# A vision tower's embedding and attention loop: pixel copies image by image, in eight pieces on ScalarE and VectorE instead of three on ScalarE and GpSimd

## The reference

```python
def _L0_tok_ref(img, w, b, patch_size):          # img: (64, 3, 224, 224)
    patches = img.reshape(B, C, Hp, p, Wp, p)    # p = 16, Hp = Wp = 14: 196 tokens an image
    patches = patches.transpose(0, 2, 4, 1, 3, 5).reshape(B, S, C * p * p)
    out = jnp.einsum('bsk,ek->bse', patches, w) + b
    return out
...
h = _L0_tok_ref(x, L0_tok_w, L0_tok_b, 16)
h = h + _L0_attn_ref(_layernorm(h, axis=-1), L0_attn_Wq, L0_attn_Wk, L0_attn_Wv)
h = h + _L0_ffn_ref(_layernorm(h, axis=-1), ...)     # top-k experts
h = h + _L1_attn_ref(_layernorm(h, axis=-1), ...)
h = h + _L1_ffn_ref(_layernorm(h, axis=-1), ...)     # routed experts
```

## Time and profile before

| | |
|---|---|
| median of 3 runs | 2328.66 us (2323.18 to 2329.88) |
| the profiled execution | 2333.29 us, span 2331.6 us |
| busy over the span | PE 79%, PEld 57%, DVE 57%, ACT 52%, POOL 50% |
| mean granted TensorE clock | 0.904 |

### The profile page before, as it was taken

One profiled execution on the slowest core, in us unless ns is written; L12 is line 12 of the kernel. 1 busy time (PEld: TensorE's weight loads), 2 busy tenths in 40 slices (PEclk: granted clock), 3 DMA queues, 4 the chain that ended last, 5 costly groups with the idle time before them and its releaser, 6 DMA issues. The chain is left out here.

```text
span 2331.6 us, 48836 instructions
## 1 busy us (share of the span) xinstructions
PE 1835.8 (79%) x12709; PEld 1328.7 (57%) x12710; DVE 1339.7 (57%) x5135; ACT 1211.4 (52%) x2915; POOL 1161.9 (50%) x1035
## 2 busy tenths in 40 slices
PE   5888888872158874998797979797988459998996
PEld 3555555551136552665565656565655359998985
DVE  3788888855541104888777777777776422222222
ACT  2555555530025432876666666666665135555553
POOL 2344444413038872245545454545454448777776
PEclk8999999985569886999999999999999679999998
DMA  9777777610014332011111111111111057776775
GB/s 205 176 191 188 189 189 189 181 29 15 19 45 71 62 46 64 23 40 41 39 34 39 35 38 35 38 35 38 34 34 29 25 118 137 134 136 122 134 134 84
DMA packets 271687, 198.98 MB, mean 85 GB/s; under 512 B 26121, under 2 KB 251947, under 8 KB 271531
## 3 DMA queue, kind: packets, MB, share of 16 engines
q1 hardware_dynamic: 221547, 161.65, 26.8%
q0 software_dynamic: 49984, 35.38, 11.0%
HBM read 144.12 MB, written 52.80 MB: 84 GB/s over the span
## 5 line engine op out<-in xcount | busy, mean ns | idle before, releaser
L2123 POOL DMA_INDIRECT out_dram<-r_yw,r_idx x212 | 328.4, 1549 | 114.9 <-issue 50.4
L2015 POOL DMA_INDIRECT rows_scratch<-routed_row,slot_u x256 | 268.8, 1050 | 124.7 <-issue 72.8
L1691 ACT ACTIVATE a_probsT<-a_p_sc 98x392 f32<-98x392 f32 x384 | 191.9, 500 | 128.0 <-PE a_p_sc L1520 108.0
L2191 ACT ACTIVATE r_hT<-r_p_up,r_b1T 128x256 f32<-128x256 f32 x424 | 190.0, 474 | 115.0 <-PE r_p_up L2165 111.6
L2152 PEld LDWEIGHTS r_p_y<-w_all,r_hT 128*128 128x128 f32 x1696 | 223.3, 192 | 11.1
L2152 PE MATMUL r_p_y<-w_all,r_hT 128*128 x1696 | 224.2, 275 | 0.0
L2165 PE MATMUL r_p_up<-r_xgT,r_w1e 128*128 128x256 f32 x848 | 220.5, 383 | 0.7 <-ACT r_xgT L2196 0.6
L1517 PE MATMUL a_p_sc<-q_head,kT 128*98 128x392 f32 x512 | 218.9, 509 | 0.5 <-ACT q_head L1718 0.5
L407 PE MATMUL p_embed<-pix,w_pix 96*128 96x392 f32 x512 | 211.1, 520 | 4.8 <-ACT pix L533 4.8
L1718 ACT ACTIVATE q_head<-qT,head_of 128x196 f32<-128x196 f32 x512 | 197.1, 467 | 0.0
L650 POOL TENSOR_SCALAR vare<-mv 98x4 f32<-98x4 f32 x64 | 27.9, 436 | 296.9 <-DVE mv L628 215.7
(11 more groups left out here) (361 smaller groups left out, 4535.0 us busy)
## 6 DMA issues: line engine op xcount, KB each, us to landing
img<-in_x_dram SPq DMA_DIRECT2D x192, 196.0 KB, 3.6
img<-in_x_dram SPq DMA_DIRECT2D x192, 189.0 KB, 3.7
r_w1e<-in_L_ffn_W_dram SPq DMA_DIRECT2D x106, 256.0 KB, 3.0
r_xg<-rows_scratch SPq DMA_DIRECT2D x106, 130.0 KB
xn_scratch<-xn SPq DMA_DIRECT2D x32, 196.0 KB
h_scratch<-h SPq DMA_DIRECT2D x32, 196.0 KB
h<-h_scratch SPq DMA_DIRECT2D x32, 196.0 KB
h3b<-h_scratch SPq DMA_DIRECT2D x32, 196.0 KB
```

Source lines behind the costliest of these rows:

```text
L1691: act.activation(probsT[:, r3, m, b * 2 * PAIR:(b + 1) * 2 * PAIR], p_sc[i % 2][:, 0:2 * PAIR], ACT.Exp).then_inc(exped, 1)
L2015: pool.indirect_dma_start(rows_dram, bass.IndirectOffsetOnAxis(ap=slot_u[:, k % 2, c, t:t + 1], axis=0), row[:, k % 2, c, t, :], None).the ...
L2123: pool.indirect_dma_start(acc_dram, bass.IndirectOffsetOnAxis(ap=idx[:, (k - 3) % 4, t:t + 1], axis=0), yw[:, (k - 3) % 4, t, :], None, co ...
L2191: act.activation(hT[:, (k - 1) % 2, f, :], p_up[f][:, 0:G], ACT.Silu, bias=b1T[:, bass.ds(e * FC + f, 1)]).then_inc(act_h, 1)
```

## The change

Each image's half of the buffer is loaded by itself, with a semaphore of its own. The pixel copies are done image by image, in pairs of columns: eight pieces of 2 x 196 elements a unit. ScalarE does pairs 0 and 1 of each image, VectorE pairs 2 and 3; GpSimd does none. The pieces stand between the other work of these engines. TensorE's `patch` waits for all eight pieces of the unit each time that it is called. On ScalarE `hT` moves ahead of the exponentials. VectorE's `emit` now runs one iteration longer, since its pieces are of the unit ahead, and GpSimd's one shorter.

```diff
-        def load_images(sp, u, k):
-            for m in range(2):
-                dst = img[:, k % 2, m, :].rearrange("r (g w) -> r g w", g=GRID)
...
+        img_loaded = [[sem(f"img_loaded{k}_{m}") for m in range(2)] for k in range(2)]
+        def load_image(sp, u, k, m):
...
@@ emit_sp
-                    wait(sp, pix_ready, n - 1, apart=True)
-                    wait(sp, pix_ready_pool, 2 * (n - 1))
-                    load_images(sp, n, k)
+                    for m in range(2):
+                        copied = PAIRS * (n - 2) + 2 * (m + 1)
+                        wait(sp, pix_act, copied, apart=True)
+                        wait(sp, pix_dve, copied)
+                        load_image(sp, n, k, m)
@@ patch
                 if 0 in js:
-                    wait(pe, pix_ready, n + 1)
                     wait(pe, hT_ready, n)
-                if half // 2 in js:
-                    wait(pe, pix_ready_pool, 2 * n + 2)
+                wait(pe, pix_act, PAIRS * (n + 1))
+                wait(pe, pix_dve, PAIRS * (n + 1))
@@ new, called by emit_act and emit_dve
+        def copied_pixels(copy, eng, done_sem, n, k, m, pair):
+            if not live(n, 0, UNITS):
+                return
+            if pair % 2 == 0:
+                wait(eng, img_loaded[k % 2][m], (n // 2 + 1) * 16 * 6 if isinstance(n, int) else
+                     (n - (k % 2)) * (16 * 3) + 16 * 6, apart=True)
+                wait(eng, embedded, n - 1, apart=True)
+            js, q = slice(2 * pair, 2 * pair + 2), slice(m * TOKENS, (m + 1) * TOKENS)
+            in_columns = img[:, k % 2, m].rearrange("r (q j) -> r j q", j=PATCH)
+            copy(pix[:, k % 2, js, q], in_columns[:, js, :]).then_inc(done_sem, 1)
@@ emit_dve, ahead of the wait for rstd
+                pixels(ahead, k_ahead, 0, 2)
+                pixels(ahead, k_ahead, 0, 3)
@@ emit_dve, ahead of the wait for rstd2
+                pixels(ahead, k_ahead, 1, 2)
+                pixels(ahead, k_ahead, 1, 3)
@@ emit_pool
-                        js = slice(half // 2 + 2 * part, half // 2 + 2 * part + 2)
-                        pool.tensor_copy(pix[:, k_ahead % 2, js, :], by_column(k_ahead, js)).then_inc(pix_ready_pool, 1)
```

More of the change, by code:

```diff
@@ L254, in embed_and_attend @@
         n_loads = 6
-        img_loaded = [sem(f"img_loaded{k}") for k in range(2)]
+        img_loaded = [[sem(f"img_loaded{k}_{m}") for m in range(2)] for k in range(2)]
         imgs = x.rearrange("b c (g p) w -> b c p g w", p=PATCH)
-        def load_images(sp, u, k):
-            for m in range(2):
-                dst = img[:, k % 2, m, :].rearrange("r (g w) -> r g w", g=GRID)
[L262 to L266, removed]
+        def load_image(sp, u, k, m):
+            dst = img[:, k % 2, m, :].rearrange("r (g w) -> r g w", g=GRID)
+            for c in range(CHANNELS):
+                lo, hi = (slice(CHANNELS * s + c, 2 * rows, 2 * CHANNELS) for s in range(2))
+                sp.dma_start(dst[lo], imgs[2 * u + m, c]).then_inc(img_loaded[k % 2][m], 16)
+                sp.dma_start(dst[hi, :, 0:SIDE - half], imgs[2 * u + m, c, :, :, half:]
+                             ).then_inc(img_loaded[k % 2][m], 16)
         def load_weights(sp):
@@ L506, in emit_pe, with pixels @@
             software_pipeline(pe, emit, DEPTH, UNROLL, UNITS)
[L508 to L514, removed]
+        def copied_pixels(copy, eng, done_sem, n, k, m, pair):
[8 more added lines that the diff above has]
+            copy(pix[:, k % 2, js, q], in_columns[:, js, :]).then_inc(done_sem, 1)
         def emit_act(act):
+            def pixels(n, k, m, pair):
+                copied_pixels(act.copy, act, pix_act, n, k, m, pair)
             def emit(ahead, k_ahead):
@@ L523, in emit @@
                     act.copy(hcur[:, (k - 1) % 4], p_htr[:]).then_inc(h_ready, 1)
+                pixels(ahead, k_ahead, 0, 0)
                 if live(n, 2, UNITS):
@@ L527, in emit @@
                     act.copy(xdT[:, (k - 2) % 2, :], p_tr[:, 0:COLS]).then_inc(xdT_ready, 1)
+                pixels(ahead, k_ahead, 0, 1)
+                if live(n, 2, UNITS):
+                    u = n - 2
                     wait(act, u_ready, u + 1)
                     act.mul(uT[:, (k - 2) % 2, :], p_mm[:, 0:COLS], score_scale[:, 0:1]).then_inc(uT_ready, 1)
[L530 to L533, removed]
+                pixels(ahead, k_ahead, 1, 0)
                 if live(n, 4, UNITS):
@@ L556, in emit @@
                                            ).then_inc(exp_ready, 1)
[L557 to L561, removed]
                 if live(n, 4, UNITS):
@@ L573, in emit_dve, with pixels, emit @@
         def emit_dve(dve):
-            def emit(n, k):
+            def pixels(n, k, m, pair):
+                copied_pixels(dve.tensor_copy, dve, pix_dve, n, k, m, pair)
+            def emit(ahead, k_ahead):
+                n, k = ahead - 1, k_ahead - 1
                 if live(n, 1, UNITS):
@@ L637, in emit @@
                     assert st.k == H2_STEPS, st.k
-            software_pipeline(dve, emit, DEPTH, UNROLL, UNITS)
+            software_pipeline(dve, emit, DEPTH + 1, UNROLL, UNITS)
         def emit_pool(pool):
-            def emit(ahead, k_ahead):
-                n, k = ahead - 1, k_ahead - 1
-                for part, (skew, step, at, m, v, r, ready, per) in enumerate((
+            def emit(n, k):
+                for skew, step, at, m, v, r, ready, per in (
                         (1, ln_step, 8, mv, vare, rstd, rstd_ready, LN_STEPS),
-                        (3, h2_step, 13, mv2, vare2, rstd2, rstd2_ready, H2_STEPS))):
+                        (3, h2_step, 13, mv2, vare2, rstd2, rstd2_ready, H2_STEPS)):
                     if live(n, skew, UNITS):
```

21 lines of the change are left out of this document (15 added, 6 removed).

## The result

The changed kernel takes 2337.25 us (median of 13 runs, 2327.53 to 2347.27) against 2327.35 us of the kernel before on the same chip: a ratio of 1.0049, interval 1.0029 to 1.0069. It is slower by half a percent; 2306 us had been forecast. The profiled execution has a span of 2344.5 us, 12.9 above the one before (both lie above their medians, by 9 and 6 us).

The account below looks back on a forecast made before the run. GpSimd's pixel copies were taken to hold VectorE, which sets the 14.63 us unit. 26 units at 13.9 us save 19 us and both ends 4, together 23 off the median 2328.7: 2306 us, range 2294 to 2326.

Parts of the forecast that it names:

- What bounds the kernel: VectorE sets the pace of the loop's 14.63 us unit; GpSimd's pixel copies hold it for 2.73 us a unit.
- The pieces: VectorE's four pixel copies a unit: 0.52 us each, 0.96 a pair, plus 0.24 of waits a pair.
- the cheap: Rival on VectorE's pixel copies: 0.36 us a piece, a unit of 13.6, 2298 us in all; chance 0.13.
- the dear case: Rival on VectorE's pixel copies: 0.75 us a piece, a unit of 14.36, 2318 us in all; chance 0.14.
- The new wait of TensorE: At its first embedding matmul TensorE waits about 1.7 us a unit for VectorE's last pair of pieces.
- The ring: Chain from `rinv` through VectorE's last pair and TensorE's matmuls back to `rinv`: 13.9 us a unit.
- ScalarE's ring: Chain from the embedding's end through ScalarE's work and a piece back to it: 13.2 us, shorter than the binding chain.
- `hT` ahead of the exponentials: On ScalarE, costs nothing in its chain in the loop; gives about 1.4 us once in ramp and once in drain.
- Loads by image: SyncE's split image loads cost and bring nothing in the loop; image 1 has a slack of 0.9 us at worst.
- Both ends together: Start and end of the kernel, from earlier image copies and `hT`: 4 us saved in all.
- The sum: Over the loop, 26 x (14.63 - 13.9) = 19 us saved; with 4 at both ends, 23 us.
- The rival on the port: VectorE's last pair stands behind GpSimd's `vare` and power: a unit of 15.2 us, 2339 us in all; chance 0.10.

Follow-up runs that it names:

- e5: The changed kernel with 40 instructions (80 fulfilled waits) put ahead of VectorE's loop, none in it; 0.9973 of the kernel before.
- e7: e5 with TensorE's first embedding matmul waiting only for ScalarE's pieces and the fifth for VectorE's; 0.9782 of the kernel before.
- e4: The changed kernel with all 32 units of VectorE's program written out, without a loop; 0.9862 of the kernel before.
- e10: e5 with `hT` put behind the four exponentials again; 0.9920 of the kernel before.
- e11: e5 with both images of a unit under one semaphore again, loaded behind the unit's last copy; 1.0013 of the kernel before.
- e8: e4 with TensorE's first embedding matmul waiting only for ScalarE's pieces and the fifth for VectorE's; 0.9791 of the kernel before.
- e9: The changed kernel, loop not moved, with TensorE waiting for VectorE's pieces only at the fifth embedding matmul; 0.9912 of the kernel before.
- e6: e2 with 32 more instructions of fulfilled waits ahead of VectorE's loop; 1.0067 of the kernel before.
- e2: The kernel before with 32 more fulfilled waits in VectorE's loop body, 299 instructions instead of 267; 1.0020 of the kernel before.
- e3: The kernel before with 16 more fulfilled waits in VectorE's loop body, 283 instructions; 1.0003 of the kernel before.

## Why the prediction was wrong, step by step

**What bounds the kernel: right.** GpSimd's copies held VectorE. Without them `amax * rstd` is 0.18 (0.16 forecast) and VectorE stopped being the bound.

**The pieces: right.** 0.496 us in the median against 0.52, 0.91 to 0.93 a pair against 0.96, the idle ahead of a pair 0.29 and 0.30 against 0.24. Neither the cheap nor the dear case came. The estimate of 0.36 rests on the two elements a cycle of the Trainium skill ("VectorE: DVE Perf Modes", § Mode 2×_2P) and the fixed 150 cycles that the same page gives in § Side-by-side: where the cycles go for N=2048 bf16; for these copies it is too low by 0.14. No run here tells whether they ran in that mode.

**The new wait of TensorE: right, in kind and size.** 1.7 us forecast, 1.61 to 1.72 in the loop of e5. e7 shows that it holds the unit. The ring was worked out as 13.9; undisturbed units of e5 take 14.0 to 14.1. Written out (e4) they take 13.5: there the semaphore steps that stand in the loop ahead of the aggregates and of the last pair (0.16 and 0.30 on the ring) are absent. I had priced such waits, but not seen that leaving the loop would save them all.

**ScalarE's ring: sound.** 13.2 was worked out; with TensorE's wait gone (e7) a unit takes 13.07. That the two agree doesn't show that this ring holds e7: its small waits are for `xdT`, `xn` and images. At this pace ScalarE does wait for images, where the prediction left image 1 a slack of 0.9 at worst.

**`hT` ahead of the exponentials: right**, nothing in the loop (e10).

**Loads by image "cost and bring nothing in the loop": half wrong.** In the changed kernel ScalarE never waits for an image in the loop, so nothing was lost. But undoing it costs 0.57 us a unit and 8.7 at the start (e11; about 3 of the latter can be scatter), since the pieces now begin right behind `hcur`, where the copy before stood behind `uT`. The early pieces need the split loads (or their earlier issue; e11 undoes both together); I had judged it against the place of the copy before. Both ends together: 4 forecast, 6.1 at the start alone.

**The sum: here it failed.** "26 x (14.63 - 13.9) = 19" takes each unit of the loop as undisturbed. In its place stands 26 x (14.63 - 15.32) = -18. Of the 1.42 us between 13.9 and 15.32, moving the loop alone takes back 1.04 (e5 against the changed kernel, 14.28 and 15.32). Of the remaining 0.38, the five units of e5 at half clock, 1.7 above 13.9, make 0.32, its eighteen undisturbed ones, 0.15 above, make 0.10, and three of 13.5 take 0.04 back. The first term was missing altogether: what VectorE needs to get its own instructions. Its size is that of one execution each. The ratios say less: from 1.0049 to 0.9973 is 0.0076, 17.7 us, or 0.68 a unit if all of it lies there. And by its median e5 gains 5.5 us of the 23 forecast: without the stall the change gains, but not what was forecast, and where the rest went is shown only as far as the five units go. The written-out start shifted by 16 rows (323 to 307, since `emit` now runs one unit ahead) and the body grew by 30, and so the loop came to pass three marks instead of two. The order of the instructions on VectorE was looked at for what stands beside what, not for where the loop lies. The profile before could not have shown a stall; the rows of fetches in its ramp, and the length of the loop against their distance, would have made it a rival.

The Trainium skill does have a rule on this that was passed over: "Runtime: NRT & Kernel Launch", § Instruction fetch mechanics, says that a taken branch to a place outside the instructions held forces a transfer before the engine goes on, in blocks of 16 KiB of which two are held. This case agrees with the stall behind the branch, but its transfers are of 8192 bytes, for about 128 instructions, half of the page's blocks. A loop that touches three such pieces stays, one that touches four does not, if the marks are the pieces' borders; by the page's 32 KiB four would still be held, which the runs don't show. No run here tells borders from middles.

**The half clock** comes on top. It was no term of the prediction, which took the 1.00 of the earlier trace rows over. Its share of the 1.04 is not shown by itself, since the stretches follow the stalls: 47.8 us of them in the changed kernel, 17.1 in e5. What has a price is one stretch of 3.4 us in e5, a unit of 15.5 in place of 14.05. By it the 30.7 us more would be nine such stretches and 0.5 us a unit, and the idle of VectorE behind the five branches (17.9 us) 0.7 a unit; both are estimates, and as they add to more than 1.04 they overlap.

**The rival on the port** gave 2339 us for another reason, and was close by accident. GpSimd's power did become longer beside VectorE's pieces, but by 0.15 on the mean, not by the length of the pair. Power and pieces run at the same time (222.03 to 223.42 and 222.87 to 223.80), so the exclusion that the Trainium skill names ("SBUF — State Buffer", § Who interferes with whom) is not what happens between these two instructions; whether the pieces ran in a two-port mode no run here shows. The groups of GpSimd from 91 to 471 us, before and after, and two powers of one unit:

```profile
L652 POOL TENSOR_TENSOR rstd<-vare,halfpow 98x4 f32<-98x4 f32 x52 | 53.9, 1037 | 4.3
```

```profile
L673 POOL TENSOR_TENSOR rstd<-vare,halfpow 98x4 f32<-98x4 f32 x49 | 58.2, 1189 | 4.1
```

```profile
217.48 1.19 POOL L673 TENSOR_TENSOR rstd<-vare,halfpow 98x4 f32<-98x4 f32 x1
...
222.03 1.39 POOL L673 TENSOR_TENSOR rstd<-vare,halfpow 98x4 f32<-98x4 f32 x1
```

**What was not tried:** moving the loop of the changed kernel with shorter filling than 40 instructions, a stall without a fall of the clock or the reverse, and the four kernels of the best figures on one chip. e7 and e8, both near 0.98, can't be told apart.

## What to carry to other kernels

Where an edit adds, removes or skews instructions on an engine that runs a long unrolled loop, look in the trace for instruction transfers behind its branch, and count where the loop begins and ends against their distance; a loop that only just fits is made slower by an edit that is right in all else. Here moving it by 40 instructions took the ratio from 1.0049 to 0.9973, and moving it by 112 brought the fetches back. Read the units one by one before averaging them: a mean of 15.3 here was 14.1 with 15.5s and 18s in between. When a copy is taken off one engine to end a wait, ask which consumer is the first to wait for all pieces; here waiting at the fifth matmul in place of the first was worth more than the change itself.

## What was not expected of the hardware

- Instructions come in transfers of 8192 bytes, about one for 128 instructions of VectorE (e4: at its rows 577, 700, 839, 953, 1095, 1214, 1334, 1477). A loop of 299 instructions at rows 387 to 686 needs none, one of 289 at rows 305 to 594 needs five a pass, and three of these, in the changed kernel 2.6 to 3.4 us apart, hold VectorE 2.1 to 3.5 and 1.1 to 1.6 us behind the branch (the changed kernel and e9).
- TensorE's clock halves in the loop of e5 for 3.4 us about every fifth unit, where TensorE waits 1.6 to 1.7 us at one place of each unit; such a stretch costs 1.5 us. With the stalls (the changed kernel, e6, e9) the stretches are 3.4 to 10.2 us. The kernel before, with waits of 1.30 and 0.75 in a unit, e2 with 1.4 to 1.5 (once 1.75), e4 with 1.04 to 1.14, and e7, with 0.41 and 0.18 in the unit shown, keep the full clock in these units. Why 1.6 is dearer than 1.5 no run shows.
- Fulfilled waits on VectorE are nearly free: eight instructions of them a unit made a unit of the kernel before 0.15 us longer (e2), four made it no longer (e3).
- A GpSimd power of 98x4 elements takes 1.04 us in the kernel before and 1.39 in the row shown beside VectorE's strided copies.
